# Adding the rotated query halves on VectorE before one transpose per block, in a fused GAT + attention + expert kernel

## The chip, the cores and the metric

One NeuronCore of a Trainium2 chip runs the whole program, written as five hand-ordered instruction streams: TensorE (PE), VectorE (DVE), ScalarE (ACT), GpSimd (POOL) and SyncE (SP). The metric is the device time of one execution in microseconds; the median of three runs of the kernel before is 664.06 us.

## The reference

For each of 4 batches of 256 rows of width 256, two graph-attention layers are followed by one transformer block with 16 query heads and 4 key heads of size 128 and 8 experts, top 2. The part that the change touches is how queries are rotated:

```python
def apply_rope(x, cos, sin):
    half = x.shape[-1] // 2
    x1, x2 = (x[..., :half], x[..., half:])
    return jnp.concatenate([x1 * c - x2 * s, x2 * c + x1 * s], axis=-1)
...
x = x + gat(ctx_512, layernorm(x))          # two GAT layers, mask from layernorm(x)
h = rmsnorm(layernorm(x), attn_norm_w)      # 256 x 256 per batch
q = rope(rmsnorm(h @ q_w.T))                # 16 heads of 128
k = rope(rmsnorm(h @ k_w.T)); v = h @ v_w.T # 4 heads of 128
attn = softmax(causal(q @ k.T * scale)) @ v
hidden = h_in + attn @ o_w.T                # then rmsnorm, gate, 8 experts (silu), top 2
```

## The kernel before

**Order.** Every engine walks the same list, PLAN. Each of the four batches has a "tail" (the transformer block) of 48 steps. Beside the tail of batch b run the graph layers of batch b + 2 ("gat") and the norm of batch b + 1 ("prep"), step by step: in a step, gat comes first, then prep, then tail. So the tails of batches 0 and 1 are interleaved with graph work, and those of batches 2 and 3 are not. Which item of a tail stands in which step is written out by hand in tables (QKV_AT, TURN_AT, SCORE_AT, ...). Within a step the tail's items come in the order of KINDS: qkv, turn, score, probT, av, ... On DVE and POOL some work comes after all items of the step: on DVE the reciprocals of the softmax sums (table SUM_AT), on POOL the scaling of the probabilities with them (function normalise).

**A block of queries.** The projections come in blocks of 128 rows by 512 columns (4 heads). There are 12 a batch: two of keys, two of values, eight of queries. The ten of keys and queries are units u = 0..9 (u = 0, 1 the keys). A query unit u goes through these hands:

1. PE projects it into a PSUM bank (L559, two matmuls of 128x512 over a contraction of 256; the trace counts each as two, so a block is "x4").
2. ACT copies it to `raw` (L707, tile "early") and writes its square (L708), which frees the bank.
3. DVE multiplies it by the cosine table into `m1[:, u % 4]` (L1020) and sums the squares per head (L1023).
4. POOL multiplies the swapped halves by the sine table into `m2[:, u % 4]` (L836, two instructions).
5. PE "turns" it: for each of 4 heads a transpose of the m1 part (L567) and one of the m2 part (L568) accumulate in one PSUM bank, so the addition of the two products is done by PE. For keys DVE adds m1 and m2 (L1036), scales them (L1041), and PE makes one transpose a head (L565).
6. ACT copies the turned block to `qT` (L716).

After u = 1, 5 and 9 DVE makes the first guess of an inverse root (L1029 to L1031) and POOL refines it by three Newton steps in 12 small instructions (L772 to L776) and, for queries, one scaling (L822).

**Scores.** Score n = 3g + j is made on PE (L573, with the causal mask added by L575) from head group g. DVE takes the row maximum (L1051) and its negative product with the inverse root (L1052). ACT exponentiates (L726). DVE makes the reciprocal (L1123), POOL scales the probabilities (L852), PE transposes them (probT: L580, L584) and multiplies by the values (L588, L592). PE needs turn 2g + 2 or 2g + 3 for a score. Scores share two PSUM banks (0 and 1) with other slow work; projections, turns and probT share three (2 to 4), given out in turn in PE's order.

**Waits.** m1[u % 4] and m2[u % 4] are reused every four units: DVE and POOL wait until the turn of unit u - 4 has filled its bank. PE in a turn waits for m1 and m2 of the unit:

```python
if kind == "turn":
    if n < T:
        pe.wait_ge(k_ready, (b + 1) * T)
    else:
        pe.wait_ge(m1_ready, b * QU + n + 4)
        pe.wait_ge(m2_ready, b * QU + n + 4)
```

## Time and profile before

| what | value |
|---|---|
| three runs, median (lowest to highest) | 664.06 us (659.31 to 664.84) |
| the profiled execution, its own time | 662.46 us |
| its span in the trace | 660.7 us |
| mean granted TensorE clock | 0.977 of full speed |
| PE / PE weight loads busy | 606.6 us (92%) / 437.0 us |
| DVE / POOL / ACT busy | 434.6 / 305.9 / 268.6 us |
| chain that ended last | PE 64%, DVE 20%, issue 6%, POOL 4%, ACT 4% |

Busy time of PE overlaps weight loads with matmuls, and the end of a matmul is modelled: neighbouring matmuls start closer together than one lasts. The distance from one start to the next is what an instruction takes of PE's time. The clock column of a stretch is the granted TensorE clock: 1.00 is 2.4 GHz, 0.50 is 1.2 GHz.

### The profile page before, as it was taken

To read this page: it belongs to the slowest core of one execution; us is meant where nothing else is said; L and a number is where in the kernel's file an instruction comes from. 1 tells how busy PE (TensorE), PEld (TensorE's weight loads), DVE (VectorE), ACT (ScalarE), POOL (GpSimd) and SP (SyncE) were. 2 spreads that over 40 slices of the span, in tenths; PEclk is the share of its full clock that TensorE was granted. 3 is DMA by queue.
4 is the path that set the end of the run, shared out by engine and by line. 5 is a ranking of instruction groups with operands and counts; after the bars stand their busy time and mean duration, and the time that the engine had idled before them with its cause. 6 is when DMAs were issued, how large, how long until landed. Compare 5 with 4: busy or idle time off the path is not lost.

```text
span 660.7 us, 10362 instructions
## 1 busy us (share of the span) xinstructions
PE 606.6 (92%) x3271; PEld 437.0 (66%) x3271; DVE 434.6 (66%) x1279; ACT 268.6 (41%) x653; POOL 305.9 (46%) x588
## 2 busy tenths in 40 slices
PE   3799899489799999989799999989999998999998
PEld 2278468236586789736597789746768873666886
DVE  4997499389756387689757387655653656664463
ACT  2462563065566333055556333036750204675020
POOL 1493594278853240268854150267730027863000
PEclk9999899799999999998989999999999999999999
DMA  8920000000000000000000000000000000000000
GB/s 276 387 73 2 1 1 4 12 4 2 1 1 0 1 2 1 24 9 1 0 2 1 0 1 1 3 15 1 1 1 0 1 9 8 1 0 1 1 0 17
DMA packets 8729, 14.41 MB, mean 22 GB/s; under 512 B 908, under 2 KB 7372, under 8 KB 8420
## 3 DMA queue, kind: packets, MB, share of 16 engines
q1 hardware_dynamic: 8676, 13.76, 5.9%
q8 instruction: 27, 0.44, 0.3%
q14 instruction: 26, 0.21, 0.1%
HBM read 12.70 MB, written 1.05 MB: 21 GB/s over the span
## 4 chain that ended last, share of the span: by engine, by line
PE 64%; DVE 20%; issue 6%; POOL 4%; ACT 4%; DMA 1%; DVEq 0%; POOLq 0%; SPq 0%; ACTq 0%
PE bank L615 14%; PE bank L513 10%; PE bank L573 6%; PE bank L559 5%; PE bank L592 4%; PE ob L487 4%; PE tb L476 3%; PE bank L637 2%; DVE tt L958 2%; PE bank L588 2%; PE bank L584 2%; DVE ssq L1023 2%; ACT prob L726 2%; DVE m L1020 2%; DVE qT L958 1%
## 5 line engine op out<-in xcount | busy, mean ns | idle before, releaser
L559 PE MATMUL bank<-wqkv_sb,hT 128*128 128x512 f32 x192 | 95.0, 635 | 0.4 <-ACT v_sb L702 0.4
L726 ACT ACTIVATE prob<-bank,sneg,rms 128x128 f32<-128x128 f32 (+1 forms) x128 | 63.9, 508 | 59.6 <-DVE sneg L1052 59.4
L836 POOL TENSOR_TENSOR m<-early,rope_s 128x256 f32<-128x256 f32 x80 | 73.5, 942 | 30.8 <-ACT early L707 30.6
L513 PE MATMUL bank<-m,wgu_sb 128*128 128x128 f32 (+1 forms) x480 | 85.6, 329 | 0.8 <-DVE early L1099 0.8
L794 POOL TENSOR_SCALAR tt<-tt,gmn 128x256 f32<-128x256 f32 x96 | 67.3, 710 | 37.4 <-DVE gmn L958 37.0
L852 POOL TENSOR_SCALAR prob<-prob,srcp 128x128 f32<-128x128 f32 (+1 forms) x128 | 53.1, 432 | 51.4 <-DVE srcp L1123 51.2
L513 PEld LDWEIGHTS bank<-m,wgu_sb 128*128 128x128 f32 x480 | 71.0, 191 | 9.0 <-DVE early L1099 2.2
L573 PE MATMUL bank<-kT,qT 128*128 128x128 f32 (+1 forms) x256 | 61.5, 356 | 1.8 <-ACT prob L726 1.8
L559 PEld LDWEIGHTS bank<-wqkv_sb,hT 128*128 128x128 f32 x192 | 35.9, 199 | 36.9 <-issue 34.0
L615 PE MATMUL bank<-wo_sb,qT 128*128 128x256 f32 x256 | 59.0, 382 | 0.7 <-ACT qT L732 0.7
L707 ACT ACTIVATE early<-bank 128x512 f32<-128x512 f32 x40 | 24.1, 602 | 84.4 <-PE bank L559 84.4
L1051 DVE TENSOR_REDUCE smx<-bank 128x2 f32<-128x512 f32 (+1 forms) x48 | 33.0, 687 | 32.6 <-PE bank L575 29.9
L615 PEld LDWEIGHTS bank<-wo_sb,qT 128*128 128x128 f32 x256 | 47.5, 190 | 10.0 <-issue 4.4
L573 PEld LDWEIGHTS bank<-kT,qT 128*128 128x128 f32 x256 | 41.6, 199 | 14.1 <-issue 5.7
L949 DVE SCALAR_TENSOR_TENSOR lr<-zs 128x512 f32<-128x512 f32 x48 | 35.5, 740 | 18.9 <-ACT zs L685 18.2
L487 PEld LDWEIGHTS ob<-feat,gpT 128*128 128x128 f32 x384 | 47.0, 192 | 1.2 <-issue 0.8
L487 PE MATMUL ob<-feat,gpT 128*128 128x33 f32 x384 | 47.1, 267 | 0.4 <-DVE rows L967 0.3
L958 DVE CUSTOM_DVE_ANT_0 tt<-lr,maskv 128x256 f32<-128x256 f32 x96 | 46.6, 520 | 0.0
L685 ACT ACTIVATE zs<-zb 128x512 f32<-128x512 f32 x48 | 28.7, 598 | 41.8 <-PE zb L468 41.6
L1020 DVE TENSOR_TENSOR m<-early,rope_c 128x512 f32<-128x512 f32 x40 | 29.4, 735 | 21.6 <-ACT early L707 21.5
L742 ACT ACTIVATE pT<-bank 128x256 f32<-128x256 f32 x44 | 16.9, 383 | 58.8 <-PE bank L513 46.4
L772 POOL TENSOR_TENSOR ln_a<-ln_y 128x4 f32<-128x4 f32 x12 | 2.4, 199 | 82.8 <-DVEq L996 82.2
(200 smaller groups left out, 1217.0 us busy)
## 6 DMA issues: line engine op xcount, KB each, us to landing
wqkv_sb<-wqkv_dram SPq DMA_DIRECT2D x1, 3072.0 KB, 12.0
wgu_sb<-wgu_dram SPq DMA_DIRECT2D x2, 1408.0 KB, 11.5
wo_sb<-wo_dram SPq DMA_DIRECT2D x1, 2048.0 KB, 18.2
wd_sb<-wd_dram SPq DMA_DIRECT2D x1, 1408.0 KB, 15.6
out_dram<-rows SPq DMA_DIRECT2D x8, 128.0 KB, 1.7
xin<-x_dram SPq DMA_DIRECT2D x3, 256.0 KB, 2.7
rows<-gat_rows_dram SPq DMA_DIRECT2D x2, 256.0 KB, 2.8
kT<-x_dram SPq DMA_DIRECT2D x1, 256.0 KB, 4.5
```

Source lines behind the costliest of these rows:

```text
L487: mm = pe.matmul(ob[i][:, hh * FE:(hh + 1) * FE], gpT[i][:, k % 3, h, m, :], feat[i][:, m, hh, :], start=(m == 0), stop=(m == T - 1))
L513: mm = pe.matmul(ps[:, m * N + c0:m * N + c1], wgu_sb[:, m, k, n * P:(n + 1) * P], tokT[:, k, c0:c1], start=(k == 0), stop=(k == KT - 1))
L559: mm = pe.matmul(ps[:, :], hT[:, k, t * P:(t + 1) * P], wqkv_sb[:, k, c * G * HD:(c + 1) * G * HD], start=(k == 0), stop=(k == KT - 1))
L573: pe.matmul(ps[:, i * nk:(i + 1) * nk], qT[:, G * g + h, t * P:(t + 1) * P], kT[:, g, 0:nk], start=True, stop=False)
L615: mm = pe.matmul(bank_of(w)[:, 0:D], lhs[:, k, t * P:(t + 1) * P], rhs[:, k, :], start=(k == 0), stop=(k == end - 1))
L726: ins = act.activation(prob[:, n % 5, i * nk:(i + 1) * nk], ps[:, i * nk:(i + 1) * nk], ACT.Exp, bias=sneg[:, n, i:i + 1], scale=rq(g, t, ...
L794: ins = pool.tensor_scalar(tt[i][:, k % 3, h, :], tt[i][:, k % 3, h, :], -1.0, gmn[i][:, k % 3, h:h + 1], ALU.mult, ALU.add)
L836: ins = pool.tensor_tensor(dst[:, :, c, :], src[:, :, 1 - c, :], s_, ALU.mult)
L852: ins = pool.tensor_scalar(part_, part_, srcp[:, n, i:i + 1], 1.0, ALU.mult, ALU.mult)
L949: dve.scalar_tensor_tensor(lr[i][:, k % 2, :], zs[i][:, k % 2, :], 0.2, zs[i][:, k % 2, :], ALU.mult, ALU.min)\
L958: ins = dve.tensor_tensor_reduce(tt[i][:, k % 3, h, :], lr[i][:, k % 2, h * N:(h + 1) * N], maskv[i][:, t, :], 1.0, 3e38, ALU.add, ALU.min ...
L1020: ins = dve.tensor_tensor(m1[:, u % 4, :].rearrange("p (h d) -> p h d", h=G), raw[:, u % 3, :].rearrange("p (h d) -> p h d", h=G), c_, ALU ...
```

## The change

DVE now adds m1 and m2 of each query unit (function rope_sums), after the other items of the step given by SUMMED_AT, and counts them in a new semaphore rope_ready. A turn of queries is one transpose a head, and waits for rope_ready; it stands two steps behind its addition. The last projection (qkv 11) leaves step 11 for step 12. POOL may write m2 again once the addition has read it. Because turns and projections share three banks in PE's order, the banks of steps 8 to 16 are given out anew.

```diff
-QKV_AT = (1, 2, 3, 4, 5, 6, 7, 8, 9, 10, 11, 11)
-TURN_AT = (6, 7, 8, 9, 10, 11, 11, 12, 13, 14)
+QKV_AT = (1, 2, 3, 4, 5, 6, 7, 8, 9, 10, 11, 12)
+TURN_AT = (6, 7, 9, 10, 11, 12, 13, 14, 15, 16)
+SUMMED_AT = (7, 8, 9, 10, 11, 12, 13, 14)
...
-                        pe.wait_ge(m1_ready, b * QU + n + 4)
-                        pe.wait_ge(m2_ready, b * QU + n + 4)
+                        pe.wait_ge(rope_ready, b * len(SUMMED_AT) + n - 1)
...
-                        if n < T:
-                            mm = pe.transpose(dst, m1[:, n % 4, src], ident)
-                        else:
-                            pe.matmul(dst, m1[:, n % 4, src], ident, is_transpose=True, start=True, stop=False)
-                            mm = pe.matmul(dst, m2[:, n % 4, src], ident, is_transpose=True, start=False, stop=True)
+                        mm = pe.transpose(dst, m1[:, n % 4, src], ident)
...
-                    if u >= 4:
-                        filled(pool, b, ("turn", u - 4))
+                    if u >= 6:
+                        pool.wait_ge(rope_ready, b * len(SUMMED_AT) + u - 5)
+                    elif u >= 4:
+                        pool.wait_ge(k_ready, (b + 1) * T)
...
+            def rope_sums(b, s):
+
+                for u in [n + 2 for n, at in enumerate(SUMMED_AT) if at == s]:
+                    dve.wait_ge(m2_ready, b * QU + u + 4)
+                    dve.wait_ge(m1_ready, b * QU + u + 4)
+                    dve.nop(nofuse=True)
+                    dve.tensor_tensor(m1[:, u % 4, :], m1[:, u % 4, :], m2[:, u % 4, :], ALU.add).then_inc(rope_ready, 1)
...
                         part(b, w)
+                    rope_sums(b, s)
```

How the streams stand in the tail of batch 3, steps 11 to 12. In the names, m1 and m2 are the two products, early is raw or its square, smx and sneg are the maxima of a score, rms is the inverse root. First DVE, before:

```order
L1020 TENSOR_TENSOR m1<-early,rope_c 128x512
L1023 TENSOR_REDUCE ssq<-early 128x4
L1020 TENSOR_TENSOR m1<-early,rope_c 128x512
L1023 TENSOR_REDUCE ssq<-early 128x4
L1029 TENSOR_SCALAR ssq<-ssq 128x16
L1030 TENSOR_SCALAR rms_a<-ssq 128x16
L1031 TENSOR_SCALAR rms<-rms_a 128x16
L1051 TENSOR_REDUCE smx<-bank0 128x2
L1052 SCALAR_TENSOR_TENSOR sneg<-smx,rms 128x2
L1051 TENSOR_REDUCE smx<-bank1 128x2
L1052 SCALAR_TENSOR_TENSOR sneg<-smx,rms 128x2
```

and the same place after the change:

```order
L1019 TENSOR_TENSOR m1<-early,rope_c 128x512
L1022 TENSOR_REDUCE ssq<-early 128x4
L1050 TENSOR_REDUCE smx<-bank0 128x2
L1051 SCALAR_TENSOR_TENSOR sneg<-smx,rms 128x2
L1124 TENSOR_TENSOR m1<-m1,m2 128x512
L1019 TENSOR_TENSOR m1<-early,rope_c 128x512
L1022 TENSOR_REDUCE ssq<-early 128x4
L1028 TENSOR_SCALAR ssq<-ssq 128x16
L1029 TENSOR_SCALAR rms_a<-ssq 128x16
L1030 TENSOR_SCALAR rms<-rms_a 128x16
L1050 TENSOR_REDUCE smx<-bank1 128x2
L1051 SCALAR_TENSOR_TENSOR sneg<-smx,rms 128x2
```

The maximum of score 1 now stands ahead of the last unit's product and guess, and an addition stands between them. ACT at the same place, before:

```order
L726 ACTIVATE prob,ssum<-bank1,sneg,rms 128x128 x4
L707 ACTIVATE early<-bank3 128x512
L708 ACTIVATE early<-bank3 128x512
L707 ACTIVATE early<-bank4 128x512
L708 ACTIVATE early<-bank4 128x512
L716 ACTIVATE qT<-bank2 128x4x128
L716 ACTIVATE qT<-bank3 128x4x128
L726 ACTIVATE prob,ssum<-bank0,sneg,rms 128x256 x2
```

and after:

```order
L723 ACTIVATE prob,ssum<-bank1,sneg,rms 128x128 x4
L704 ACTIVATE early<-bank2 128x512
L705 ACTIVATE early<-bank2 128x512
L713 ACTIVATE qT<-bank3 128x4x128
L723 ACTIVATE prob,ssum<-bank0,sneg,rms 128x256 x2
L704 ACTIVATE early<-bank4 128x512
L705 ACTIVATE early<-bank4 128x512
L713 ACTIVATE qT<-bank2 128x4x128
```

The last unit's copy and square (the second pair of "early") moved behind the exponentials of score 1. PE around the first transpose of probabilities (probT 0, step 14), after the change:

```order
L565 MATMUL bank4<-cst,m1 128x128 x4
L570 MATMUL bank1<-kT,qT 128x256
L572 MATMUL bank1<-causal,identb 128x128
L570 MATMUL bank1<-kT,qT 128x256
L572 MATMUL bank1<-causal,identb 128x128
L577 MATMUL bank2<-cst,prob 128x128 x4
L565 MATMUL bank3<-cst,m1 128x128 x4
L570 MATMUL bank0<-kT,qT 128x256
L572 MATMUL bank0<-causal,identb 128x128
```

Turn 7 stands ahead of probT 0 (L577) and turns 8 and 9 behind it; in the kernel before, all turns stood ahead of it.

## Rows read from the trace of the kernel before

**Rows 1.** The page's first part: busy time, share of the span and instructions by engine.

```profile
PE 606.6 (92%) x3271; PEld 437.0 (66%) x3271; DVE 434.6 (66%) x1279; ACT 268.6 (41%) x653; POOL 305.9 (46%) x588
```

**Rows 2.** PE's timeline, one turn, batch 3: start, length, instruction, count.

```profile
562.56 0.27 PE L567 MATMUL bank<-cst,m 128*128 128x128 f32 x1
...
563.43 1.88 PE L559 MATMUL bank<-wqkv_sb,hT 128*128 128x512 f32 x4
```

**Rows 3.** PE's timeline, batch 3, steps 13 to 15; in brackets the idle time before.

```profile
580.18 0.49 PE L573 MATMUL bank<-kT,qT 128*128 128x128 f32 x2 [0.67 <-ACT prob L726]
...
583.81 0.66 PE L580 MATMUL bank<-cst,prob 128*128 128x128 f32 x4 [0.17 <-POOL prob L852]
584.68 0.70 PE L573 MATMUL bank<-kT,qT 128*128 128x256 f32 x2 [0.21 <-ACT prob L726]
```

**Rows 4.** ACT's timeline, batch 3, steps 11 and 12.

```profile
573.38 0.60 ACT L707 ACTIVATE early<-bank 128x512 f32<-128x512 f32 x1
...
578.93 0.56 ACT L726 ACTIVATE prob<-bank,sneg,rms 128x256 f32<-128x256 f32 x1 [2.51 <-DVE sneg L1052]
...
580.02 0.59 ACT L716 ACTIVATE qT<-bank 128x512 f32<-128x512 f32 x1
```

**Rows 5.** DVE's timeline, batch 3, steps 9 to 11.

```profile
565.98 0.69 DVE L1020 TENSOR_TENSOR m<-early,rope_c 128x512 f32<-128x512 f32 x1 [0.18 <-ACT early L707]
...
574.02 0.69 DVE L1020 TENSOR_TENSOR m<-early,rope_c 128x512 f32<-128x512 f32 x1 [2.42 <-ACT early L707]
...
575.22 0.68 DVE L1020 TENSOR_TENSOR m<-early,rope_c 128x512 f32<-128x512 f32 x1
...
576.54 0.67 DVE L1029 TENSOR_SCALAR ssq<-ssq 128x16 f32<-128x16 f32 x1
...
578.01 0.68 DVE L1051 TENSOR_REDUCE smx<-bank 128x2 f32<-128x512 f32 x1
```

**Rows 6.** POOL's timeline, batch 3, steps 8 to 13.

```profile
566.17 0.58 POOL L773 TENSOR_TENSOR rms_a<-rms_a,ssq 128x16 f32<-128x16 f32 x1
...
578.18 0.21 POOL L772 TENSOR_TENSOR rms_a<-rms 128x16 f32<-128x16 f32 x1 [0.32 <-DVE rms L1031]
...
582.35 2.32 POOL L852 TENSOR_SCALAR prob<-prob,srcp 128x128 f32<-128x128 f32 x6
```

**Rows 7.** The addition that keys already have, by line: ns minimum/median/maximum.

```profile
L1036 DVE TENSOR_TENSOR m<-m x8: 684/688/693, 142.3 to 552.3; 128x512 f32<-128x512 f32 x8
```

**Rows 8.** PE's timeline, batch 0 (with graph work), steps 13 and 14.

```profile
179.80 0.63 PE L476 MATMUL tb<-cst,tt 128*128 128x128 f32 x4 [2.74 <-ACT gpT L690]
...
188.10 0.61 PE L580 MATMUL bank<-cst,prob 128*128 128x128 f32 x4
```

**Rows 9.** DVE's timeline, batch 0, steps 10 and 11.

```profile
167.02 0.29 DVE L1052 SCALAR_TENSOR_TENSOR sneg<-smx,rms 128x4 f32<-128x4 f32 x1
...
177.28 0.16 DVE L1052 SCALAR_TENSOR_TENSOR sneg<-smx,rms 128x2 f32<-128x2 f32 x1
```

**Rows 10.** ACT's timeline, batch 0, step 11: two graph items, then a unit's copy.

```profile
169.10 0.60 ACT L685 ACTIVATE zs<-zb 128x512 f32<-128x512 f32 x1
169.57 0.61 ACT L690 ACTIVATE gpT<-tb 128x512 f32<-128x512 f32 x1
170.05 0.62 ACT L707 ACTIVATE early<-bank 128x512 f32<-128x512 f32 x1
```

**Rows 11.** Stretches of DVE: from:to length, busy (instructions), granted clock, DMA, GB/s.

```profile
147.20:165.70 18.50, 18.40 (x41) 0.91 0.01 2
```

**Rows 12.** The same for PE.

```profile
177.10:179.80 2.70, 0.00 (x1) 1.00 0.00 0
181.30:184.70 3.40, 3.40 (x18) 0.50 0.00 0
...
555.50:558.20 2.70, 0.04 (x2) 1.00 0.01 3
558.20:561.60 3.40, 3.40 (x14) 1.00 0.00 0
...
586.30:606.30 20.00, 20.00 (x110) 1.00 0.01 1
```

More of the change, by code:

```diff
@@ L121 @@
 assert MIXT_AT[0] > UPDOWN_AT[6]
+assert all(QKV_AT[n + 4] < SUMMED_AT[n] < TURN_AT[n + 2] for n in range(len(SUMMED_AT)))
 def work(s):
@@ L324, in block_program @@
         free = [sem(f"free{k}") for k in range(BANKS)]
-        raw_ready, m1_ready, m2_ready = sem("raw_ready"), sem("m1_ready"), sem("m2_ready")
+        raw_ready, m1_ready, m2_ready, rope_ready = sem("raw_ready"), sem("m1_ready"), sem("m2_ready"), sem("rope_ready")
         k_ready, seed_ready, rms_ready, pool_b = sem("k_ready"), sem("seed_ready"), sem("rms_ready"), sem("pool_b")
```

## The prediction

> **What bounds the kernel now.** I read the page first. PE is busy 92% of a span of 660.7 us, DVE 66%, POOL 46% [rows 1]. By that alone this is a PE kernel, and a change that takes 128 transposes off PE and puts 32 additions on DVE should pay. But such shares are means over stages. So I next read PE's timeline through steps 8 to 16 of a tail, where the change acts, and asked at each wait who ends it. In the tail of batch 3, which has no graph work beside it, PE waits only 0.67, 0.17 and 0.21 us in steps 13 to 15 [rows 3], but all of these waits are ended by ACT and POOL, at the end of a long chain over several engines. The chain is: the exponentials of score 0 end on ACT; ACT copies the next unit; DVE multiplies it, sums its squares, makes the guess; DVE takes the maximum of score 1; ACT exponentiates; POOL refines the inverse root and only then scales the probabilities; PE transposes them. PE and this chain are level in the kernel before. The reader is to see in rows 4 to 6 that the chain has almost no air in it. Taking work off PE there gives nothing unless the chain gets shorter as well.
>
> **The gain on PE.** In a turn the starts are 0.11 us apart, and eight of them take 562.56 to 563.43 = 0.87 us [rows 2]. Half goes: 0.435 us a turn, 32 turns, 13.9 us in all. It is an upper bound as long as PE's waits stay what they are; without PE's other waits it could reach a little further (rival 1).
>
> **What DVE gets.** An addition of this very shape exists for keys and takes 0.688 us [rows 7]; started back to back it costs about 0.61. 32 x 0.61 = 19.5 us of DVE. Where DVE waits anyway it is free: in batch 3 DVE sat idle 2.42 us before unit 8 [rows 5]. Where it is in the chain it is not.
>
> **The tail without graph work (batches 2 and 3), link by link.** All is counted from 573.38, when ACT has finished score 0's exponentials [rows 4]. This start does not move by the change: it hangs on the inverse root of units 2 to 5, whose guess still follows unit 5's raw, and the first addition (0.61) falls before unit 5's raw is there (unit 4 is done early enough on DVE). From 573.38 to probT 0 at 583.81 [rows 3] is 10.43 us now. After the change, step 11 has only unit 8, and unit 9 comes in step 12, on ACT behind score 1's exponentials and on POOL with its Newton steps still ahead of the scaling:
> - ACT's copy of unit 8 until DVE starts on it: 573.38 to 574.02 = 0.64 [rows 4, 5];
> - DVE's product and squares: 1.20 (574.02 to 575.22) [rows 5], and 0.08 for the hand-over to the next;
> - maximum of score 1 until ACT's exponentials start: 578.01 to 578.93 = 0.92 [rows 4, 5];
> - two exponentials: 578.93 to 580.02 = 1.09 [rows 4];
> - copy, product and squares of unit 9: again 0.64 + 1.28;
> - its guess: 576.54 to 578.10, which is 1.56 [rows 5, 6];
> - Newton and the scaling to SCALE on POOL: 578.18 to 582.35 = 4.17, plus 0.08 to start [rows 6];
> - scaling of four pieces of probabilities: 2.32 / 6 = 0.39 each, 1.55, and 0.1 to PE [rows 6].
>
> The sum is 13.3 us, so probT 0 comes 2.9 us later. What score 1's maximum gains by no longer waiting for unit 9 is used up, because unit 9 now waits for score 1. The addition of unit 6 lies behind score 1's maximum and ahead of unit 9 (covered by ACT's 1.73), and the addition of unit 7 lies behind score 2: turn 7 therefore waits until about 582.1, which is hidden, since probT 0 is later still. Then two turns (units 8 and 9) that used to be ahead of probT 0 are behind it: 2 x 0.435 = 0.87. Against that the wait of 0.21 at 584.68 goes [rows 3]. Net: 2.9 + 0.87 - 0.21 = 3.5 us a tail. After this point PE runs without a wait for 20 us [rows 12], so nothing gives it back. What else the new bank turns do (turn 5 now waits for the bank of projection 10, about 1.2 us) is hidden under the same chain. Two tails: **+7.0 us**.
>
> **Bound of the POOL term.** A small instruction of the Newton steps took 0.58 us on POOL at 566.17 and its like 0.21 at 578.18 [rows 6]; the slow one began while DVE ran L1020 from 565.98 to 566.67 [rows 5]. An addition beside the Newton steps may cost POOL 0.37 so, once or twice a tail: 0 to +0.7 each, or 0 to +2.9 in all; below zero it can't go, since nothing is taken from DVE there. I take 0 and keep the upper end. The Trainium skill ("SBUF — State Buffer", "SBUF: two separate sides") says that DVE with two SBUF inputs and a GpSimd instruction exclude each other for the whole instruction; the trace agrees, as far as one pair shows it, and by the rule all 32 additions would be such intruders: 32 x 0.69 = 22 us of blocked port, an upper bound that the sum does without since most lie where POOL has slack.
>
> **The tails with graph work (batches 0 and 1).** Here the same chain sets PE's wait of 2.74 us, since the ACT work that ends it stands behind score 1's exponentials [rows 8], and now the change cuts both ways. DVE has no idle time from 147.2 to 165.7 us [rows 11], so two additions (7, 8) come in ahead of the guess and of unit 7, and score 0's negative maximum moves from 167.3 to about 168.6, +1.3 [rows 9]. Between score 0 and score 1 one unit and the guess leave: 1.2 + 1.6 (as in batch 3) and 0.4 for their slower run beside POOL, an estimate, = 3.2 us earlier, less the 1.3: score 1's comes at about 175.5 in place of 177.4 [rows 9]. The wait of 2.74 shrinks to about 1. Then unit 9 follows on ACT behind the exponentials and two graph items (1.09 + 0.95 + 0.64 [rows 10]), on DVE graph work 0.6 (an estimate), then 1.28 + 1.56, Newton 4.25 and 0.4 for graph work beside it, scaling 1.65: 175.5 + 12.5 = 188.0, against 188.10 now [rows 8]. With the two turns behind it (0.87): +0.8. Since score 3 and turn 8 ran at half clock before [rows 12] and may not after, which gives up to 1.7 back, I take **0 for each**, with -2 and +2 as ends.
>
> **The clock.** After a wait of 2.74 us in batch 0 the granted clock is 0.50 for 3.4 us (181.3 to 184.7), but after one of 2.7 us in batch 3 it stays at 1.00 [rows 8, 12]. At 1.2 GHz such a stretch does 1.7 us less work. In tails 2 and 3 the change makes two new waits of PE, before turn 7 and before probT 0, about 3.5 and 2.7 us, 1.7 us apart. I count one stretch at half clock in the full part behind them: 1.7 each, **+3.4**. In tails 0 and 1 a stretch is there already, and is dealt with above. The Trainium skill ("TensorE: Matmul & The Clock Gate", "Part 1: The HAM clock gate") has it that idleness throttles the array to 1.2 GHz; by it, a rival would be that idleness in smaller pieces does so as well.
>
> **Sum.** 7.0 + 0 + 3.4 = +10.4 us. On the profiled execution's 662.46 us that is 672.9; it lies 1.6 us under the median of 664.06, within the spread of the runs (659.31 to 664.84), so I put the difference on the median: **674.5 us**, 1.6% slower. About 1% is what a measurement of this kernel tells from no change, so the bounds of "same" are 657.4 and 670.7.
>
> **Rivals.**
> - *1. PE is the bound (faster).* If turns cost the path what the page suggests, -13.9, and the waits of 2.74 us in tails 0 and 1 shrink by 0.5 each: 649 us. For it: 92% and hardly a wait. Against: every wait in steps 11 to 15 is ended by ACT or POOL. It wins if unit 9's place on ACT does not matter, that is if score 1's exponentials end before projection 11 does. Chance 0.11.
> - *2. The shorter way to score 1 wins (same).* In tails 0 and 1 the wait of 2.74 goes altogether and with it the stretch at half clock: -2.7 - 1.7 = -4.4 each, -8.8 in two, against +7.0 and perhaps the clock: 662 to 666, say 664. For it: both are in the trace. Chance 0.24.
> - *3. The mechanism holds, but the clock does not fall:* 671. Chance 0.20.
> - *4. DVE becomes the bound where it is full.* Then all additions up to step 11 (five of 0.61 to 0.7) lie on the way in tails 0 and 1: +3.3 each on top of the forecast, 681. It decides if graph work has no slack towards DVE in steps 7 to 10. Chance 0.08.
> - *My forecast,* 674.5, takes 0.37. That the change is not what it says can't be: the order of the streams shows it.
>
> **Range and chances.** 657 to 680: below lies rival 1 with a little of 2, above lies rival 4. Slower by over 1%: the forecast, over half of rival 3, and rival 4, 0.57. Within 1%: rival 2 and the rest of 3, 0.30. Faster: 0.13.
>
> **What would show it.** In PE's timeline of batch 3, probT 0 should start some 2.9 us later after ACT's score 0 than before, released by POOL (the scaling), with a wait of about 3.5 us ahead of turn 7 released by DVE's addition. ACT's copy of the last unit should wait behind two exponentials. In batches 0 and 1 the wait of 2.74 should be about 1. PE's busy time should be some 14 us less while the span is not. Wrong would be: probT 0 unmoved in batch 3; or PE continuous through steps 11 to 15, in which case rival 1 holds.

## The result, and the profile after

The changed kernel takes 684.22 us (median of 5 runs, 681.17 to 684.78) against 664.84 us (659.31 to 665.09): a ratio of 1.0301 with a 95% interval of 1.0256 to 1.0346. It is slower, as forecast, but by 19.4 us and not by 10.4, and it lies outside the range. The profiled executions, 681.17 and 662.46 us, differ by 18.7 us. One execution of one experiment (the changed kernel with both deferrals) took 773.9 us at a mean granted clock of 0.749, against 673.2 to 673.8 in its other three, and is left out of its ratio.

The page's first part (busy time, share, instructions by engine), of the changed kernel:

```profile
span 679.4 us, 10170 instructions
PE 606.3 (89%) x3143; PEld 430.0 (63%) x3143; DVE 454.5 (67%) x1311; ACT 269.5 (40%) x653; POOL 315.4 (46%) x588
```

128 matmuls are gone, yet PE's busy time, 606.3 us, is unchanged against [rows 1] (606.6). The mean granted clock fell from 0.977 of 660.7 us to 0.957 of 679.4 us; with two levels, 1.2 and 2.4 GHz, that is about 30 us at the lower one before (2 x 0.023 x 660.7) and 58 us now. 28 us more at half clock do 14 us less work, which is the size of the 13.9 us that the change takes off PE. DVE has 19.9 us more, where the additions should take 19.5. POOL has 9.5 us more for the same 588 instructions; nothing in its own code explains that, and the run with one input below does.

PE's timeline of batch 3, steps 12 to 15 (start, length, instruction, idle time before), answers to [rows 3]:

```profile
588.49 0.63 PE L565 MATMUL bank<-cst,m 128*128 128x128 f32 x4 [2.07 <-ACT early L705]
...
590.66 0.66 PE L565 MATMUL bank<-cst,m 128*128 128x128 f32 x4 [0.52 <-DVE m L1124]
...
595.62 0.66 PE L565 MATMUL bank<-cst,m 128*128 128x128 f32 x4 [2.82 <-DVE m L1124]
...
600.65 0.96 PE L577 MATMUL bank<-cst,prob 128*128 128x128 f32 x4 [3.14 <-POOL prob L851]
601.40 1.06 PE L565 MATMUL bank<-cst,m 128*128 128x128 f32 x4
```

The first transpose of probabilities (L577) waits 3.14 us for POOL's scaling, turn 7 waits 2.82 us for its addition, turn 5 waits 2.07 us for the bank of projection 10. ACT's timeline in the same place answers to [rows 4]:

```profile
587.26 0.60 ACT L704 ACTIVATE early<-bank 128x512 f32<-128x512 f32 x1
...
590.01 0.56 ACT L723 ACTIVATE prob<-bank,sneg,rms 128x256 f32<-128x256 f32 x1 [1.18 <-DVE sneg L1051]
590.56 0.56 ACT L723 ACTIVATE prob<-bank,sneg,rms 128x256 f32<-128x256 f32 x1
591.11 0.59 ACT L704 ACTIVATE early<-bank 128x512 f32<-128x512 f32 x1
```

DVE's timeline there, answering to [rows 5]:

```profile
584.58 0.69 DVE L1050 TENSOR_REDUCE smx<-bank 128x4 f32<-128x512 f32 x1 [2.13 <-POOL rms L819]
...
591.73 0.69 DVE L1019 TENSOR_TENSOR m<-early,rope_c 128x512 f32<-128x512 f32 x1 [1.12 <-ACT early L704]
...
593.05 0.67 DVE L1028 TENSOR_SCALAR ssq<-ssq 128x16 f32<-128x16 f32 x1
...
594.87 0.69 DVE L1124 TENSOR_TENSOR m<-m 128x512 f32<-128x512 f32 x1
```

POOL's timeline there, answering to [rows 6]:

```profile
580.57 0.74 POOL L773 TENSOR_TENSOR rms<-rms,rms_a 128x16 f32<-128x16 f32 x1
...
594.22 0.22 POOL L769 TENSOR_TENSOR rms_a<-rms 128x16 f32<-128x16 f32 x1 [0.53 <-DVE rms L1030]
...
599.18 2.33 POOL L851 TENSOR_SCALAR prob<-prob,srcp 128x128 f32<-128x128 f32 x6
```

The chain can be read off: ACT's copy of unit 9 (591.11) stands behind score 1's exponentials, DVE's product follows at 591.73, the guess at 593.05, POOL's Newton steps run from 594.22 to 599.1, and only then comes the scaling.

Stretches of PE (from:to length, busy, granted clock), answering to [rows 12]:

```profile
184.50:191.20 6.70, 6.01 (x26) 0.50 0.01 2
600.90:604.30 3.40, 3.40 (x15) 0.50 0.00 0
606.00:626.00 20.00, 19.70 (x109) 1.00 0.01 2
```

In batch 0 the clock is at 1.2 GHz for 6.7 us where it was 3.4. PE still waits there ahead of a graph layer's transposes, answering to [rows 8]:

```profile
171.83 0.39 PE L470 MATMUL zb<-pair_r,pair_l 48*128 48x512 bf16 x1 [2.35 <-ACT zs L682]
...
185.19 1.09 PE L478 MATMUL tb<-cst,tt 128*128 128x128 f32 x4 [3.07 <-ACT gpT L687]
...
190.55 0.95 PE L577 MATMUL bank<-cst,prob 128*128 128x128 f32 x4
```

It is not the same wait as before. The one of 2.74 us ended with the graph item behind score 1's exponentials; it is gone in batch 0 and 1.8 us in batch 1. This one stands a step later. DVE's and ACT's timelines of batch 0 show what sets it:

```profile
181.89 0.65 DVE L1030 TENSOR_SCALAR rms<-rms_a 128x16 int32<-128x16 int32 x1
182.45 0.68 DVE L1050 TENSOR_REDUCE smx<-bank 128x2 f32<-128x512 f32 x1
...
183.36 0.56 ACT L723 ACTIVATE prob<-bank,sneg,rms 128x256 f32<-128x256 f32 x1 [3.11 <-DVE sneg L1051]
...
184.46 0.59 ACT L687 ACTIVATE gpT<-tb 128x512 f32<-128x512 f32 x1
```

Unit 9's guess (L1030 is its end) now stands ahead of score 2's maximum on DVE, so score 2's exponentials and the graph item behind them on ACT come late, and PE waits for that item.

To say where time goes I cut each tail at four landmarks, from the starts in PE's and ACT's timelines: its first projection (a), score 0's first exponential (b), the first transpose of probabilities (c), the first product with the values (d). The length of a whole tail runs to the next one's first projection, or to the end. In us:

| kernel | batch | a to b | b to c | c to d | whole tail |
|---|---|---|---|---|---|
| before | 0 / 1 | 38.8 / 36.7 | 20.8 / 20.8 | 3.3 / 3.3 | 152.3 / 149.5 |
| before | 2 / 3 | 28.2 / 26.6 | 12.2 / 12.2 | 2.4 / 2.4 | 114.7 / 115.6 |
| after | 0 / 1 | 40.1 / 38.2 | 21.1 / 21.1 | 4.0 / 4.2 | 155.1 / 152.8 |
| after | 2 / 3 | 29.3 / 27.6 | 15.2 / 15.2 | 3.9 / 4.1 | 120.7 / 121.5 |

So batches 2 and 3 lose 6.0 and 5.9 us, batches 0 and 1 lose 2.8 and 3.2, and 0.8 us lies ahead of batch 0, where the code is the same. The sum is 18.7. a to b of batches 2 and 3 differ by 1.7 in either kernel because of the clock after PE's wait for the keys: in the profiled executions it falls in batch 2 and not in batch 3. Such differences set how far one profile can be read. a of batch 0 lies between 127.8 and 130.7 us in the kernels below, and a to b of batch 0 is 38.8 us in the kernel before but 40.6 in the one with only the last projection moved, whose code is the same up to b. a to b of batch 1 is 36.7 us in each of the eight kernels without additions (the sum over one tile, which loads DVE too, not counted), so that column is firm for batch 1 and not for batch 0.

### The profile page after: what moved, and what is told of

It is laid out like the page before. It is cut to its first block, busy times and chain, and to the rows that moved or that the text cites. A ratio compares the mean times of both kernels' runs of the same rounds, so it can differ in the third digit from the quotient of the medians.

```text
span 679.4 us, 10170 instructions
## 1 busy us (share of the span) xinstructions
PE 606.3 (89%) x3143; PEld 430.0 (63%) x3143; DVE 454.5 (67%) x1311; ACT 269.5 (40%) x653; POOL 315.4 (46%) x588
## 4 chain that ended last, share of the span: by engine, by line
PE 61%; DVE 21%; POOL 7%; issue 6%; ACT 4%; DMA 1%; DVEq 0%; POOLq 0%; SPq 0%; ACTq 0%
PE bank L612 14%; PE bank L515 9%; PE bank L570 5%; PE bank L589 4%; PE ob L489 4%; PE bank L634 4%; PE bank L560 3%; PE tb L478 3%; DVE tt L957 2%; DVE ssq L1022 2%; PE bank L581 2%; PE bank L585 2%; DVE m L1019 2%; ACT prob L723 2%; POOL rms_a L769 2%
## 5 line engine op out<-in xcount | busy, mean ns | idle before, releaser
L560 PE MATMUL bank<-wqkv_sb,hT 128*128 128x512 f32 x192 | 97.9, 649 | 0.4 <-ACT v_sb L699 0.4
L835 POOL TENSOR_TENSOR m<-early,rope_s 128x256 f32<-128x256 f32 x80 | 77.7, 995 | 32.7 <-ACT early L704 32.1
L570 PE MATMUL bank<-kT,qT 128*128 128x128 f32 (+1 forms) x256 | 63.2, 363 | 0.0
L1050 DVE TENSOR_REDUCE smx<-bank 128x2 f32<-128x512 f32 (+1 forms) x48 | 32.9, 686 | 32.9 <-PE bank L572 28.3
L489 PEld LDWEIGHTS ob<-feat,gpT 128*128 128x128 f32 x384 | 49.5, 201 | 0.8 <-issue 0.4
L489 PE MATMUL ob<-feat,gpT 128*128 128x33 f32 x384 | 49.4, 275 | 0.0
L565 PEld LDWEIGHTS bank<-cst,m 128*128 128x128 f32 x160 | 22.0, 164 | 42.9 <-issue 15.9
L565 PE MATMUL bank<-cst,m 128*128 128x128 f32 x160 | 28.7, 308 | 22.8 <-DVE m L1040 9.9
```

The source lines that it names most:

```text
L489: mm = pe.matmul(ob[i][:, hh * FE:(hh + 1) * FE], gpT[i][:, k % 3, h, m, :], feat[i][:, m, hh, :], start=(m == 0), stop=(m == T - 1))
L560: mm = pe.matmul(ps[:, :], hT[:, k, t * P:(t + 1) * P], wqkv_sb[:, k, c * G * HD:(c + 1) * G * HD], start=(k == 0), stop=(k == KT - 1))
L565: mm = pe.transpose(dst, m1[:, n % 4, src], ident)
L570: pe.matmul(ps[:, i * nk:(i + 1) * nk], qT[:, G * g + h, t * P:(t + 1) * P], kT[:, g, 0:nk], start=True, stop=False)
L835: ins = pool.tensor_tensor(dst[:, :, c, :], src[:, :, 1 - c, :], s_, ALU.mult)
```

## The experiments

All are compared with the kernel before on the same chip. Theory A is the order of the steps (unit 9 behind score 1, the Newton steps ahead of the scaling); theory B is that the additions load DVE and hold up POOL. The clock came in as a third.

### One part done or undone

The last projection back in step 11, all else as changed:

```diff
-QKV_AT = (1, 2, 3, 4, 5, 6, 7, 8, 9, 10, 11, 12)
+QKV_AT = (1, 2, 3, 4, 5, 6, 7, 8, 9, 10, 11, 11)
```

> The changed kernel, with the last projection (and so unit 9) back in step 11; additions and turns stay where the change put them. Theory A (the way of unit 9 behind score 1 sets the first transpose of probabilities): in the tails without graph work the time from score 0's exponentials to that transpose falls from 15.1 us back to 10.5 to 12, PE's wait ahead of it (3.14 us) goes, and the kernel takes 673 to 678 us. Theory B (the additions load DVE and block POOL; the place of unit 9 does not matter): 681 to 685 us.

Measured: 676.42 us, ratio 1.0211 (1.0156 to 1.0266). b to c in batches 2 and 3 is 13.9 and 14.0 us, c to d 2.4. So A has a part of 6 to 8 us, but the way does not fall back to 12: 1.8 us of it are not unit 9's place. In batches 0 and 1 b to c is 21.7 and 21.8, 0.6 longer than in the changed kernel, and the whole tails are longer by 0.6 and 0.1: beside graph work the later step does not cost, and may save a little.

The new tables alone, in the kernel before (two transposes, no addition):

```diff
-QKV_AT = (1, 2, 3, 4, 5, 6, 7, 8, 9, 10, 11, 11)
-TURN_AT = (6, 7, 8, 9, 10, 11, 11, 12, 13, 14)
+QKV_AT = (1, 2, 3, 4, 5, 6, 7, 8, 9, 10, 11, 12)
+TURN_AT = (6, 7, 9, 10, 11, 12, 13, 14, 15, 16)
```

> The kernel before with the new tables for projections and turns, but the old turn: two transposes a head, no addition on DVE. Theory A (steps, not additions): PE's 14 us of second transposes fall mostly into its new waits, so it is nearly as slow as the changed kernel, 676 to 684 us. Theory B (additions): 662 to 668 us, as before.

Measured: 677.03 us, ratio 1.0188 (1.0166 to 1.0211), as theory A had it. Without a single addition, the order costs over three fifths of the loss. b to c is 18.9 us in batches 0 and 1 and 14.4 in batches 2 and 3, c to d 4.1 in each of the first two and 5.5 and 5.0 in the others.

One number of the kernel before changed: the last projection in step 12.

```diff
-QKV_AT = (1, 2, 3, 4, 5, 6, 7, 8, 9, 10, 11, 11)
+QKV_AT = (1, 2, 3, 4, 5, 6, 7, 8, 9, 10, 11, 12)
```

> The kernel before with one number changed: the last projection in step 12. Theory A: unit 9's chain alone costs some 3 us in each of the two tails without graph work and 0 to 2 in the others, 670 to 676 us. Theory B: within 1% of before, 662 to 667 us.

Measured: 671.01 us, ratio 1.0097 (1.0074 to 1.0121). Its b to c is 18.7 us in batches 0 and 1, 2.1 less than before, and 14.4 in batches 2 and 3, 2.2 more, the same as with all the new tables. PE's timeline in batch 3 shows the wait that came in:

```profile
587.27 0.70 PE L573 MATMUL bank<-kT,qT 128*128 128x256 f32 x2 [0.91 <-ACT prob L726]
...
590.91 1.12 PE L580 MATMUL bank<-cst,prob 128*128 128x128 f32 x4 [2.34 <-POOL prob L852]
```

The forecast's mechanism is in this kernel: unit 9's chain costs 2.2 us where there is no graph work. Rival 2's is there in part only. The wait of 2.74 us goes, but one of 1.5 and 1.7 us comes in a step later. And most of the 2.1 us are not the shorter way: in the kernel before with matmuls in the keys' wait (below), where these steps are unchanged, b to c of batches 0 and 1 is 19.15 us, because there the stretch at half clock fell 3.7 and 5.2 us behind b, ahead of PE's wait, and not behind the wait (13.9 us after b). Against that, the shorter way gives 0.45 us.

Additions and single transposes at the old steps, each addition one step behind its unit:

```diff
-QKV_AT = (1, 2, 3, 4, 5, 6, 7, 8, 9, 10, 11, 12)
-TURN_AT = (6, 7, 9, 10, 11, 12, 13, 14, 15, 16)
-SUMMED_AT = (7, 8, 9, 10, 11, 12, 13, 14)
+QKV_AT = (1, 2, 3, 4, 5, 6, 7, 8, 9, 10, 11, 11)
+TURN_AT = (6, 7, 8, 9, 10, 11, 11, 12, 13, 14)
+SUMMED_AT = (6, 7, 8, 9, 10, 11, 12, 12)
```

> The changed kernel's additions and single transposes at the old steps: projections and turns as before, each addition one step behind its unit. Theory A: additions are mostly in idle time of DVE and PE gives up 14 us, of which the chain lets a few through: 656 to 666 us. Theory B (additions cost): each addition stands ahead of a maximum or of the guess, 672 to 684 us.

Measured: 685.16 us, ratio 1.0325 (1.0287 to 1.0363), just above theory B's range. b to c is 22.9 and 22.6 us in batches 0 and 1, 16.9 and 15.9 in the others. The additions with their single transposes, at steps where all else is as before, cost as much as the whole change, so my theory A for this run was wrong. The parts do not add: the new steps cost 1.9% when they stand alone, and nothing on top of the additions, to which they give room.

### What of an addition costs

The addition left out, waits and tables kept (the queries lack their sine part):

```diff
-                    dve.nop(nofuse=True)
-                    dve.tensor_tensor(m1[:, u % 4, :], m1[:, u % 4, :], m2[:, u % 4, :], ALU.add).then_inc(rope_ready, 1)
+                    dve.sem_inc(rope_ready, 1)
```

> The changed kernel with the addition left out: the waits, the single transpose and all tables stay, DVE only counts; the queries are turned without their sine part. It tells what the 32 additions cost by themselves. Theory C (DVE is in the path in the tails with graph work, and beside the Newton steps everywhere): the time to score 0's exponentials falls by 1 to 1.4 us a tail, the rest of the tails with graph work by 2 to 3 us, and the kernel takes 666 to 672 us. Theory D (the additions fit in idle time; all of the loss is the order of the steps): 679 to 684 us.

Measured: 677.79 us, ratio 1.0195 (1.0142 to 1.0248), between the two theories. a to b of batches 1 and 2 is 36.7 and 28.4, as before the change: the additions make up all of what score 0 lost. b to c falls by 0.8 in batches 2 and 3 (to 14.35) and by 0.3 to 0.7 in the others. And it cannot be told apart from the run with the tables alone, which has 128 transposes more: 13.9 us of PE's work, taken away in this order, are worth nothing that can be measured. (The two also differ in what a turn waits for: here DVE's count, made two steps earlier, there the two products themselves.) Where they went is seen in batch 1, at the graph layer's transposes. PE's timeline with the tables alone, so with two transposes a head:

```profile
336.22 0.63 PE L476 MATMUL tb<-cst,tt 128*128 128x128 f32 x4 [1.11 <-ACT gpT L690]
...
339.48 0.66 PE L580 MATMUL bank<-cst,prob 128*128 128x128 f32 x4
```

PE's timeline in the same place of the kernel with one transpose and no addition:

```profile
337.52 1.09 PE L478 MATMUL tb<-cst,tt 128*128 128x128 f32 x4 [3.05 <-ACT gpT L687]
...
342.88 0.73 PE L577 MATMUL bank<-cst,prob 128*128 128x128 f32 x4
```

The wait is 1.9 us longer, the transposes behind it take 1.09 us in place of 0.63 (the granted clock behind it is 0.50 over 5.5 us, and 1.00 over 4.8 us in the other), and the way from there to the first transpose of probabilities is 5.4 us in place of 3.3. b to c is 20.8 us, with the second transposes 18.9. Work taken off PE became a longer wait, and a slower engine behind it. This pair is the sharpest, but the others point the same way. The wait ends 14.9 to 15.8 us after b in batches 0 and 1 of all these kernels, so the other engines set its end. Behind it PE takes 3.3 us to the first transpose of probabilities in the four tails of the two kernels with two transposes a head (tables alone, projection alone), at full clock, and 4.4 to 5.4 us in the six of the changed kernel and of the runs with no addition and with one input, where the clock fell. How long the wait itself is varies: 1.8 and 3.05 us with no addition, 2.5 and 1.4 with one input.

The same, with a sum over m1 in its place, which keeps DVE as long but reads one tile:

```diff
-                    dve.tensor_tensor(m1[:, u % 4, :], m1[:, u % 4, :], m2[:, u % 4, :], ALU.add).then_inc(rope_ready, 1)
+                    dve.tensor_reduce(junk[:, u - 2, :], m1[:, u % 4, :].rearrange("p (h d) -> p h d", h=G), AX.X, ALU.add).then_inc(rope_ready, 1)
```

> The changed kernel with each addition replaced by a sum over m1 alone into a small tile, which takes DVE the same 0.67 us but reads one tile of SBUF and not two; the queries are turned without their sine part. If DVE's time alone is the price, the kernel stays at 681 to 685 us. If the additions also hold up POOL (two inputs), POOL's small instructions beside them stay near 0.22 us, each set of Newton steps gets 0.5 to 1 us shorter, and the kernel takes 674 to 679 us.

Measured: 679.87 us, ratio 1.0234 (1.0211 to 1.0258), which lies between the two expected ranges. The landmarks part the two prices. In batches 2 and 3, b to c is 14.35 us and a to b of batch 2 is 28.3, the same as with no addition at all: there DVE's time is free, and the 1.0 and 0.8 us come with the addition's second input, through POOL. In batch 1, a to b is 37.7, between 36.7 (no addition) and 38.2 (addition): there 1.0 us is DVE's time, and 0.5 POOL's. The page's group of POOL's sine products (busy us, mean ns), in the changed kernel:

```profile
L835 POOL TENSOR_TENSOR m<-early,rope_s 128x256 f32<-128x256 f32 x80 | 77.7, 995 | 32.7 <-ACT early L704 32.1 <-POOL rms L773 0.4
```

The same group of the kernel with one input:

```profile
L836 POOL TENSOR_TENSOR m<-early,rope_s 128x256 f32<-128x256 f32 x80 | 71.6, 917 | 38.1 <-ACT early L705 37.6 <-POOL rms L774 0.4
```

The small instructions show it one by one. An addition on DVE and a Newton instruction on POOL, batch 3 of the changed kernel:

```profile
580.56 0.68 DVE L1124 TENSOR_TENSOR m<-m 128x512 f32<-128x512 f32 x1
580.57 0.74 POOL L773 TENSOR_TENSOR rms<-rms,rms_a 128x16 f32<-128x16 f32 x1
```

The cosine product on DVE and a Newton instruction on POOL, batch 3 of the kernel with one input:

```profile
578.89 0.68 DVE L1020 TENSOR_TENSOR m<-early,rope_c 128x512 f32<-128x512 f32 x1
579.11 0.53 POOL L773 TENSOR_SCALAR rms_a<-rms_a 128x16 f32<-128x16 f32 x1 [0.16 <-POOL rms_a L771]
```

In the changed kernel 28 of POOL's 104 instructions on 128x16 began while DVE was in a 128x512 instruction with two SBUF inputs: 16 beside an addition, 8 beside a cosine product, 4 beside a graph item. All 28 took 0.45 to 0.74 us and ended 0.06 to 0.08 us after DVE's; of the other 76 none took over 0.33. With one input 28 such instructions began beside the sum that replaces the addition and took 0.22 us in the mean. That run also takes away the addition's write of a whole tile, but the write is not the cause: in the kernel before with the last projection in step 12 and both deferrals, 12 began beside DVE's copy of a 128x512 block from PSUM to SBUF and took 0.21 us.

The additions of steps 8 and 9 moved out of the Newton steps' way:

```diff
-SUMMED_AT = (7, 8, 9, 10, 11, 12, 13, 14)
+SUMMED_AT = (7, 7, 10, 10, 11, 12, 13, 14)
```

> The changed kernel with the additions of steps 8 and 9 taken out of the way of the first queries' Newton steps: units 3 to 5 are added in steps 7, 10 and 10. If additions beside the Newton steps made score 0 late, the time from a tail's start to score 0's exponentials falls by about 1 us in batches 1 to 3 (38.2, 29.3 and 27.6 us now), and the kernel by 2 to 4 us: 679 to 682 us. Otherwise no change, or slower by what stands behind the two additions of step 10.

Measured: 683.68 us, ratio 1.0335 (1.0278 to 1.0392), no gain. a to b falls by 0.3 and 0.5 us in batches 1 and 2, half of what I expected at most, and in batches 2 and 3 the two additions in step 10 give it back: b to c is 15.9 there in place of 15.2.

### What of the order costs

POOL's last Newton steps behind the scaling of scores 0 and 1:

```diff
-                    if u in (1, 5, 9):
+                    if u in (1, 5):
                         inverse_rms(b, (u - 1) // 4)
...
                     normalise(b, s)
+                    if s == QKV_AT[-1] + 1:
+                        inverse_rms(b, 2)
```

> The changed kernel with one thing moved: POOL makes the last Newton steps of a batch (for head groups 2 and 3) after the scaling of scores 0 and 1, at the end of step 13, instead of ahead of it. Theory A (unit 9's chain through the Newton steps sets the first transpose of probabilities): that transpose comes some 3 us earlier in the two tails without graph work, released by PE's own order or by DVE, and 0 to 2 us earlier in the others: 672 to 678 us. If another wait is level with it, such as turn 7's wait for its addition: 680 us or more.

Measured: 676.01 us, ratio 1.0186 (1.0162 to 1.0210). b to c falls from 15.2 to 12.8 and 12.5 us in batches 2 and 3 and not at all in batches 0 and 1. PE's timeline in batch 3:

```profile
588.93 1.12 PE L565 MATMUL bank<-cst,m 128*128 128x128 f32 x4 [0.32 <-DVE m L1126]
...
593.89 0.66 PE L565 MATMUL bank<-cst,m 128*128 128x128 f32 x4 [1.81 <-DVE m L1126]
...
596.30 1.06 PE L577 MATMUL bank<-cst,prob 128*128 128x128 f32 x4
```

The first transpose of probabilities no longer waits at all; the link that I named was the last one there. In batches 0 and 1 the wait of 3.07 us behind score 2 stands as it was, since the guess still stands ahead of score 2's maximum.

The same, and DVE's guess behind score 2 and the reciprocal:

```diff
                     reciprocals(b, s)
+                    if s == QKV_AT[-1]:
+                        seeds(b, 9)
```

> As the kernel with the later Newton steps, and DVE's first guess for them after score 2 and the reciprocal, too. The guess (1.5 us) then no longer stands ahead of score 2's maximum and the addition for turn 7, whose wait of 2.8 us on PE should halve: 1 to 4 us less than with the Newton steps moved alone, 669 to 676 us.

Measured: ratio 1.0145 (1.0123 to 1.0167), three runs of 673.2 to 673.8 us. Its only trace is of the execution of 773.9 us, so it gives no landmarks; those of the same kernel with matmuls added stand at the end.

Both deferrals in the kernel before, first with the last projection in step 12, then in step 11. The edits are those of the last two diffs:

> The kernel before (two transposes a head, no additions) with the last projection in step 12 and, with it, DVE's guess for the last Newton steps after score 2 and the reciprocal, and POOL's Newton steps after the scaling of scores 0 and 1. If theory A holds, the gain of the shorter way to score 1 in the tails with graph work (2 us each, as the run with the last projection moved alone showed) is kept and its loss in the two others (2.2 us to the first transpose of probabilities, and what follows) is taken away: 655 to 663 us. If the loss there is mainly unit 9's place on ACT: 664 to 669 us.

Measured: 661.90 us (10 runs), ratio 0.9984 (0.9954 to 1.0013). b to c is 17.9 in batches 0 and 1 and 10.7 in batches 2 and 3: shorter than before everywhere. Against the projection moved alone (1.0097) the deferral is worth 7.5 us. But b to c is 2.9 us shorter in batches 0 and 1 and 1.5 in the others, 8.8 in all, and the whole tails are shorter by only 0.4, 2.5, 0.5 and 0.6: a to b of batch 0 is 2.0 longer in its profile, c to d takes 0.4 back in every batch, and the stretch behind it 0.6 in batches 2 and 3. Of the 2.9 us, 1.6 are again the place of the stretch at half clock (19.15 us with unchanged steps, below).

> The kernel before with the guess and the Newton steps of the last units moved later alone, the last projection staying in step 11. Score 1's maximum no longer stands behind the guess (1.6 to 2 us of DVE): in the tails with graph work PE's wait of 2.74 us should shrink by that, 1 to 2 us each; in the others score 1 to 3 come earlier, up to 1 us each: 658 to 663 us. If PE is the bound there: 663 to 665 us.

Measured: 664.11 us (10 runs), ratio 1.0018 (0.9983 to 1.0053), no gain, though b to c is 10.9 in batches 2 and 3. c to d grows from 2.4 to 4.3 us: PE gets to the same place earlier and has to wait there. PE's timeline of batch 3 behind the first transpose of probabilities:

```profile
585.62 0.70 PE L573 MATMUL bank<-kT,qT 128*128 128x256 f32 x2 [0.54 <-ACT prob L726]
...
588.30 0.66 PE L584 MATMUL bank<-cst,prob 128*128 128x128 f32 x4 [1.38 <-POOL prob L852]
```

The second transpose of probabilities now waits for POOL, where the Newton steps stand ahead of its scaling. The chain was moved, not shortened.

### The clock

31 small matmuls into an unused bank, ahead of three waits in batches 2 and 3:

```diff
+            FILLERS = {("turn", 5): 8, ("turn", 7): 11, ("probT", 0): 12}
...
                     for w in work(s):
+                        if b >= 2:
+                            keep_clock(FILLERS.get(w, 0), zb0)
                         fill(b, w)
```

> The changed kernel with 31 small bf16 matmuls of 0.2 us into an unused bank, in the tails without graph work only, ahead of turn 5, turn 7 and the first transpose of probabilities, where PE waits 2.07, 2.82 and 3.14 us. They change no operand. Theory of the clock: the stretch at half clock that starts at 0.2 us after that transpose (600.9 in batch 3) goes, the time from there to the first product with the values falls from 4.0 to 3.3 us in both tails, and 2 to 3 us come off the whole. If the clock costs nothing there: no change, or 0 to 1 us more.

Measured: 677.27 us, ratio 1.0217 (1.0171 to 1.0263). Work added to the engine that is busiest makes the kernel 0.8% faster than the changed kernel (1.0301). PE's timeline in batch 3 (L636 are the fillers):

```profile
590.41 2.54 PE L636 MATMUL zb<-identb 128*128 128x512 bf16 x11
593.39 0.66 PE L565 MATMUL bank<-cst,m 128*128 128x128 f32 x4 [0.44 <-DVE m L1128]
...
595.12 2.75 PE L636 MATMUL zb<-identb 128*128 128x512 bf16 x12
598.39 0.66 PE L577 MATMUL bank<-cst,prob 128*128 128x128 f32 x4 [0.52 <-POOL prob L855]
598.89 0.60 PE L565 MATMUL bank<-cst,m 128*128 128x128 f32 x4
```

b to c stays at 15.1 us, so the chain is untouched, and c to d falls from 3.9 and 4.1 to 2.4 in both tails, at full clock. That is 3.2 us in the landmarks; the ratios differ by 5.6 us. The profiled execution of the changed kernel was its fastest of five: its mean granted clock was 0.957, that of the others 0.945 to 0.952, so they have more time at half clock. With the fillers it is 0.970 to 0.977.

12 such matmuls in the wait for the keys, in every batch, in the kernel before:

```diff
                 if kind == "turn":
+                    if n == 0:
+                        pe.wait_ge(free[bk], b * FILLS[bk] + turn + 1)
+                        for _ in range(12):
+                            pe.matmul(ps[:, :], identb[:, :], identb[:, :].unsqueeze(1).broadcast_to([P, 4, P]), start=True, stop=True)
```

> The kernel before with 12 small bf16 matmuls (0.2 us each) into the bank of turn 0, made while PE waits 2.7 us for the keys in every batch. No operand changes. If the stretches at half clock that follow this wait in some executions (147.1 and 444.1 in the profiled one, none in batch 3) cost time, the kernel takes 657 to 661 us and its runs lie closer together than 659.3 to 665; if they are hidden, 662 to 665 us.

Measured: 661.33 us (12 runs, 658.87 to 667.59), ratio 0.9972 (0.9939 to 1.0005). That lies between the two expected ranges: it points the way of a gain but does not exclude none, and the runs do not lie closer together. In its profile b to c of batches 0 and 1 is 19.15 us, 1.6 less than before at the same steps: PE's wait there is 1.2 us and not 2.74, because the stretch at half clock came ahead of it.

The same in the kernel with both deferrals:

> The same 12 matmuls in the kernel with the last projection in step 12 and the guess and Newton steps deferred (no additions on DVE). Both gains should add if they are separate: 654 to 660 us, faster than before by about 1%. If the clock only falls elsewhere: 660 to 663 us.

Measured: 658.87 us (12 runs, 656.53 to 662.16), ratio 0.9935 (0.9903 to 0.9966). This is the one version whose interval lies below the kernel before, by 0.65%; it keeps both transposes a head.

All remedies in the changed kernel:

> The changed kernel with the guess and the Newton steps deferred, the 12 matmuls in the keys' wait and 8 in the wait ahead of turn 5 in the tails without graph work: all remedies for the order and for the clock, with the additions and single transposes kept. If the additions are then free, it comes to 658 to 665 us, level with the kernel before; if they cost what the run without them showed (4 to 6 us of path), 666 to 671 us.

Measured: 669.43 us (10 runs), ratio 1.0099 (1.0061 to 1.0137). b to c of batches 0 and 1 is 18.1 us, 3.0 less than in the changed kernel, where moving the Newton steps alone took nothing off: there the guess's place counts, and the clock's: the stretch at half clock behind the wait is gone too. With its order and its clock mended as far as I could, the version with additions is still 10.6 us above the best one with two transposes. The two also differ in the steps of the turns and in 8 fillers ahead of turn 5, so the 10.6 us are not the additions' price alone.

## Why the prediction was right or wrong

Two steps of the sum failed. The tails with graph work stood at "0 for each" and lost 2.8 and 3.2 us, since the forecast did not follow unit 9's guess into score 2's maximum and took no further fall of the clock. And the POOL term was taken at 0 where it cost 1.8 us in a tail without graph work. One by one:

**What bounds the kernel: right.** PE's 92% was not the bound in steps 8 to 16. The two runs with and without the second transposes at the same tables (677.0 and 677.8 us) settle rival 1: 13.9 us of PE's work were worth nothing there. Rival 1 had the waits shrink as PE's work went. In batch 1 one grew from 1.11 to 3.05 us, and the clock fell behind it. My sign that PE's busy time would fall by some 14 us failed for that reason: 606.6 became 606.3, at a lower clock.

**The tails without graph work, link by link: right in mechanism, short in size.** The chain was to bring the first transpose of probabilities 2.9 us later after score 0's exponentials; b to c grew by 2.97. It waits for POOL's scaling (3.14 us), turn 7 for its addition (2.82 where I had 3.5), ACT's copy of unit 9 stands behind two exponentials. The run with the Newton steps later took exactly this wait away. That 2.9 and 2.97 agree so well is in part luck. Two sizes inside the sum compensate: the Newton steps took 4.96 us and not 4.17, and the guess 1.1 us and not 1.56. And the order alone gives 2.2 us (b to c 14.4 with the projection or the tables moved and no addition); the other 0.8 is the second input, which the sum did not have.

**"This start does not move by the change": wrong.** Score 0's exponentials came 1.1 us later in batches 2 and 3. I had priced this as the bound of the POOL term (0 to +0.7 a tail) and taken 0; it should have been taken at its upper end or above. The runs with no addition and with one input show that it is the additions' second input, and that POOL pays another 0.8 us in b to c: 1.8 us a tail, of which the forecast had none in its sum. The rule of the Trainium skill ("SBUF — State Buffer", "SBUF: two separate sides") that I had set aside as an upper bound, that a DVE instruction with two SBUF inputs and a GpSimd instruction that reads SBUF exclude each other, points the right way. The trace agrees: 28 of 28 small POOL instructions that began beside such a 128x512 one ended just behind it. The bound that I drew from it, 22 us or 5.5 a tail, is three times what a tail without graph work paid.

**"0 for each" of the tails with graph work: wrong, and the largest miss.** They lost 2.8 and 3.2 us, 6.0 together. In batch 1 score 0 came 1.5 us later, as forecast (+1.3); the 1.3 of batch 0 is within what that column varies by at the same code. The shorter way to score 1 is there too: its exponentials start 7.2 us after score 0's in batch 0 (176.61), against 10.1 before, and the wait of 2.74 us is gone there and 1.8 us in batch 1. But b to c grew by 0.4. The forecast followed unit 9 from its guess to POOL only. On DVE the guess now also stands ahead of score 2's maximum, and PE waits 3.07 us for the graph item behind score 2's exponentials, one step later than before. Behind this wait comes the clock. Of the 2.2 us from 18.9 (the new tables with two transposes) to 21.1, the run with no addition gives 0.3 and 0.7 to the additions (batches 1 and 0) and the other 1.9 and 1.6 to the single transposes and what a turn waits for: with less work PE waited longer, and went on at half clock. POOL's last Newton steps took 5.4 us (182.61 to 188.04) for the 4.65 of the sum, but PE, at half clock from 184.4 to 191.2, reached its transpose only at 190.55, when POOL had been done since 189.5. The clock, which "is there already, and is dealt with above", got twice as long.

**The clock: right that it counts, too small.** I took one stretch of 1.7 us in each of batches 2 and 3. c to d shows 1.5 and 1.7 us of it, so these were right. The ones in batches 0 and 1 were not in the sum.

**The sum.** Forecast: 7.0 for the chain, 0 and 3.4 for the clock. Measured in the profile: batches 2 and 3 together 11.9, where the forecast had 10.4; batches 0 and 1 together 6.0, where it had 0; 0.8 ahead of them. The two turns behind the first transpose of probabilities, 0.66 a tail in the sum, show as 0.5 and 0.2 us behind d.

**The rivals.** Of rival 2's saving of 4.4 us in each of batches 0 and 1 the projection moved alone shows 0.45 that is not the clock's place: the wait goes, and a shorter one comes a step later. Rival 4 (DVE the bound where it is full) had the right place, batches 0 and 1, and the right size for its own part (+3.3 each against 2.8 and 3.2). But the agreement in size is chance. Of what score 0 lost in batch 1, 1.0 of 1.5 us was DVE's time, and the rest of the tail's loss is POOL's, the guess's place and the clock's. The range's upper end counted rival 4 at 681 as the worst case; a loss in these tails was not a rival of the forecast, it came on top of it.

## What to carry to other kernels

Before taking work off the busiest engine, ask which engine ends the last wait in that stretch; if it is a chain over the others, the saved time turns into idle time, and can bring a lower clock with it (here a wait of 1.11 us became 3.05, and 1.9 us were lost). When an instruction goes to a second engine, price it three times: its own time where that engine has no slack, its effect on an engine that runs beside it (here POOL, 1.8 us in a tail without graph work), and the order in which it pushes others back. When a unit of work moves a step, follow it on every engine it visits, and ask what now stands behind it there. A small set of serial instructions, here the 13 of the inverse root, should stand behind all work of its engine that is due sooner; but where the chain behind is level, as in the kernel before, moving it gains nothing.

## What the runs showed of the hardware that was not expected

- A DVE addition of two SBUF tiles (0.69 us) delays POOL, and a sum over one tile of the same length does not: 1.8 us a batch in the landmarks of a tail without graph work, for eight additions. Each of the 28 small POOL instructions that began beside a 128x512 DVE instruction with two SBUF inputs ended 0.06 to 0.08 us after it, taking 0.45 to 0.74 us in place of some 0.21. That holds for the cosine product too, so 12 slow ones are left in the kernel with one input.
- 31 filler matmuls, 7 us of PE's time, made the kernel 0.8% faster, by taking away stretches of 3.4 us and more at 1.2 GHz after waits of 2 to 3 us. The same wait of 2.7 us is followed by such a stretch in one batch and not in the next.
- Where such a stretch falls changes a landmark by itself: b to c of batch 0 at the same steps is 20.8 us with it behind PE's wait and 19.15 with it ahead.
- Less work on PE made a stretch longer: b to c of batch 1 is 18.9 us with two transposes a head and 20.8 with one and no addition, since PE's wait inside it grew and the clock fell to 1.2 GHz.
- Two kernels that differ in 128 transposes of 0.11 us each (1.0188 and 1.0195) cannot be told apart.
